# Expert attention: V projection moved behind the last weight transposes, and VectorE's copy of V moved last

## What is computed

```
for e in range(4):                      # experts, 12 heads of 16 each, x is 16 samples x 141 tokens x 192
    q, k, v = x @ wq[e].T, x @ wk[e].T, x @ wv[e].T      # split by heads
    scores = q @ k.T / sqrt(16), masked to 0 <= i - j < 64
    o = softmax(scores) @ v
    outs.append(o @ wo[e].T)
fused = concat(outs); result = silu(fused @ w_gate.T) * (fused @ w_up.T)
```

## Time and profile before

| | us |
|---|---|
| median of 3 runs | 1338.97 (1335.55 to 1340.47) |
| profiled execution, its own time | 1340.07 |
| its span, first to last instruction | 1338.3 |
| TensorE busy: matmuls, weight loads | 1199.4, 972.4 |
| ScalarE, VectorE, GpSimd busy | 769.5, 711.5, 349.3 |
| expert attention, about | 632 to 1208 of the span |

### The profile page before, as it was taken

One profiled execution on the slowest core, in us unless ns is written; L12 is line 12 of the kernel. 1 busy time (PEld: TensorE's weight loads), 2 busy tenths in 40 slices (PEclk: granted clock), 3 DMA queues, 4 the chain that ended last, 5 costly groups with the idle time before them and its releaser, 6 DMA issues. The chain is left out here.

```text
span 1338.3 us, 34162 instructions
## 1 busy us (share of the span) xinstructions
PE 1199.4 (90%) x13220; PEld 972.4 (73%) x13220; DVE 711.5 (53%) x2290; ACT 769.5 (57%) x3346; POOL 349.3 (26%) x477
## 2 busy tenths in 40 slices
PE   6789976999997789996899999999999999995898
PEld 5479944777774456653788888988888888983465
DVE  7344465666666110023666667666666667666100
ACT  2155525677773533302877777777777777773432
POOL 2100023333332000002334433444334433441000
PEclk9789966999996799976999999999999999996799
DMA  7000000000006200001000000000000000000000
GB/s 234 20 1 1 2 1 1 1 2 2 2 2 140 44 1 1 0 1 41 2 2 2 3 2 2 2 3 2 2 2 2 2 2 3 2 2 1 9 19 27
DMA packets 34734, 19.85 MB, mean 15 GB/s; under 512 B 24592, under 2 KB 32016, under 8 KB 34576
## 3 DMA queue, kind: packets, MB, share of 16 engines
q1 hardware_dynamic: 34432, 17.20, 4.8%
q10 hardware_dynamic: 144, 0.49, 0.1%
HBM read 15.12 MB, written 1.77 MB: 13 GB/s over the span
## 5 line engine op out<-in xcount | busy, mean ns | idle before, releaser
L1692 POOL TENSOR_TENSOR e_W<-e_W,e_RS 128x384 f32<-128x384 f32 x256 | 203.8, 827 | 349.6 <-DVE e_RS L1620 349.6
L1563 ACT ACTIVATE e_W<-banks,e_MX 128x128 f32<-128x128 f32 x768 | 268.9, 389 | 18.3 <-DVE e_MX L1608 18.2
L1563 ACT ACTIVATION_READ_ACCUMULATOR e_W<-banks,e_MX 128x1 f32 x768 | 176.1, 229 | 0.0
L1557 ACT COPY e_PT<-banks 128x512 f32<-128x512 f32 x128 | 69.0, 588 | 105.0 <-PE banks L1468 105.0
L1420 PE MATMUL banks<-XT,e_wqk 128*128 128x141 f32 x768 | 112.2, 297 | 11.9 <-DVE e_GU L1662 8.4
L469 POOL TENSOR_TENSOR rstd<-veps,nhalf 128x6 f32<-128x6 f32 x15 | 20.6, 1373 | 365.8 <-DVE veps L435 365.8
L1420 PEld LDWEIGHTS banks<-XT,e_wqk 128*128 128x128 f32 x768 | 98.5, 194 | 14.3 <-issue 11.6
L1468 PE MATMUL banks<-ident,e_W 128*128 128x128 f32 x768 | 105.5, 273 | 2.7 <-POOL e_W L1692 1.6
L1432 PE MATMUL banks<-e_wv,XT 128*128 128x192 f32 (+1 forms) x512 | 100.2, 339 | 0.3 <-ACT e_K L1552 0.2
L1468 PEld LDWEIGHTS banks<-ident,e_W 128*128 128x128 f32 x768 | 90.3, 141 | 6.2 <-POOL e_W L1692 1.9
L1608 DVE TENSOR_REDUCE e_MX<-banks 128x3 f32<-128x384 f32 x128 | 65.4, 553 | 42.8 <-PE banks L1456 42.8
(11 more groups left out here) (245 smaller groups left out, 2743.2 us busy)
## 6 DMA issues: line engine op xcount, KB each, us to landing
xp<-in_patches_dram SPq DMA_DIRECT2D x4, 768.0 KB, 8.2
H<-in_h_dram SPq DMA_DIRECT2D x1, 1728.0 KB, 10.3
out_dram<-H SPq DMA_DIRECT2D x6, 288.0 KB, 2.3
e_g<-in_e_gu_dram SPq DMA_DIRECT2D x1, 1536.0 KB, 8.3
e_o<-in_e_o_dram SPq DMA_DIRECT2D x4, 192.0 KB, 5.9
e_wqk<-in_e_qk_dram SPq DMA_DIRECT2D x8, 96.0 KB, 2.6
e_wqk<-in_e_qk_dram SPq DMA_DIRECT2D x24, 32.0 KB, 2.3
e_wv<-in_e_v_dram SPq DMA_DIRECT2D x4, 192.0 KB, 2.6
```

Source lines behind the costliest of these rows:

```text
L1557: nc.scalar.copy(PT[:, 4 * u:4 * u + 4, :], bank[4 + u][:, 0:4 * P]).then_inc(s_pa, 1)
L1563: ex = nc.scalar.activation(W[n % 2][:, t, :], bank[i][:, x * P:(x + 1) * P], ACT.Exp, bias=MX[:, t:t + 1], accum_out=SM[n % 2][:, t:t + 1])
L1692: nc.gpsimd.tensor_tensor(x, x, RS[n % 2][:, 3 * i:3 * i + 3].unsqueeze(2).broadcast_to([P, 3, P]), ALU.mult).then_inc(s_nm, 1)
```

## The change

On TensorE, project_v(n) moves from directly behind scores(n) to behind transpose(n-1, 2) and transpose_tail(n-1). On VectorE, evacuate_v(n) moves from directly behind maxima(n) to behind the first reciprocal, and evacuate_tail(n-1) moves ahead of that reciprocal.

```diff
@@ TensorE @@
                         if n < N:
                             scores(n)
-                            project_v(n)
                         if 1 <= n <= N:
                             pe.wait_ge(s_pa, 2 * n - 1)
                             pe.wait_ge(s_nm, 5 * n - 1)
...
                             pe.wait_ge(s_pa, 2 * n)
                             pe.wait_ge(s_nm, 5 * n)
                             transpose_tail(n - 1)
+                        if n < N:
+                            project_v(n)
                         if n >= 2:
                             out_project(n - 2)
@@ VectorE @@
                         if n < N:
                             maxima(n)
-                            evacuate_v(n)
                         if 1 <= n <= N:
                             evacuate_weights(n - 1)
+                            evacuate_tail(n - 1)
                         if n < N:
                             reciprocals(n, 0, 6, 2)
-                        if 1 <= n <= N:
-                            evacuate_tail(n - 1)
+                            evacuate_v(n)
                         if n >= 5 and n % EXPERTS == 1:
                             copy_out((n - 5) // EXPERTS)
```

## The result

The changed kernel takes 1319.93 us (median of 4 runs, 1318.65 to 1320.78) against 1337.26 (4 runs); the ratio is 0.9869 with a 95% interval of 0.9841 to 0.9896. That is 17.5 us less by the ratio. Of these 3 us, 1.7 come from the kernel before, whose median is now 1337.26 and was 1338.97 when the range was counted from it. The profiled execution took 1320.78 us, its span 1319.1 (1338.3 before).

A forecast was written before the change was run, and what follows sets the result against it. TensorE was taken to set the pace, so only its pauses could be won: 30 even iterates by 0.35 (10.5) plus 0.6 at the start, 11.1 us, from median 1338.97 to 1327.9 us; range 1323.3 to 1333.

The forecast's parts named there:

- The wait for e_PTT: Attended products wait for VectorE's tail-weights copy; removing this was to gain 0.35 us per even iterate.
- the 0.14 us gap: Between out projection's last load and attended loads: remains with nothing awaited, cutting the even iterate's gain from 0.50 to 0.35 us.
- the slower rival: V's later copies hold up the q/k projection: 22 us more, time 1361; chance 0.04.
- The bound of 0.4 us: Iterate 0's q/k projection, delayed by V's copies, stays covered by the first transposes' wait: charged 0, at most 0.4.
- priced at 0.6: Iterate 1, without out projection, waits 1.21 us for the tail's copy, which comes 0.62 us sooner: 0.6 us gained.
- Iterate 62's gain: Expected lost, because in the last scored iterate, 63, the second transposes already wait for e_ON.
- the block between 904.04 and 905.98: TensorE's V, third set and tail, permuted: zero net, 0.05 us either way per iterate, 3.1 us over 62.
- e_K no longer releases V: Sign to look for: V's projection, moved back on TensorE, no longer starts on the end of k's copies; no size given.
- The bound of 0.05: Uncertainty for new block neighbours on TensorE: 0.05 us either way per iterate, 3.1 us over 62.
- None shows less than no gap: Reading of the nearest trace rows for the new seams on TensorE, used to take zero net cost.
- The cap: Second transposes wait for VectorE's copy e_ON: at most 0.40 us per even iterate; as rival, 6.6 us gained, 1332.4, chance 0.11.
- the range's best case: Low end of the range: even iterates at 0.40 us (12.6) with 3.1 from the seams, 1323.3 us.

The follow-up runs named there:

- the changed kernel's second profile: The changed kernel itself, unaltered, timed once more beside the kernel with VectorE's copy e_ON moved ahead: 1319.58 us, ratio 0.9868.
- the bank freed: Kernel before, with half of k's last copy taken from SBUF instead of PSUM and V's projection waiting only for the two bank-reading copies: 1335.45 us, ratio 0.9972.
- e_ON first: Changed kernel, with VectorE's copy e_ON of the attended values moved ahead of the reciprocal of the tail's sums: 1315.24 us, ratio 0.9841.
- the bank freed with VectorE's order: Kernel before, with VectorE's new order and V's PSUM bank freed one copy earlier, TensorE's order as before: 1325.01 us, ratio 0.9896.

## Why the prediction was wrong

**Direction, mechanism and most steps held.** The wait for e_PTT went from 32 times to iterate 1 and the 0.14 us gap in its place was measured in the even iterate. The Trainium skill's rule of a drain at a change of tiling mode (TensorEngine Tiling (Array Packing), Key Properties) agrees with that gap: it stands in the odd iterates before (in the even ones the longer wait covered it) and in both kinds after. The trace does not show that the rule is the cause: the change back, from the 32-column tiles to the full-array q/k projection, leaves 0.02 us (881.59 + 0.52 = 882.11, then 882.13), and no run took the 0.14 away. V's copies came 0.8 us ahead of the q/k projection, 0.9 was worked out: the slower rival was far off. Iterate 0 cost 0.01 us, charged 0, and here luck had a part. In the changed kernel's second profile its q/k projection, behind the same pause of 3.00 us, ran at a granted clock of 0.50, the 1.2 GHz level, for 2.85 us instead of 1.50, and the masks of iterate 1 came 10.91 us behind those of iterate 0 instead of 9.40. There the projection before it had run at 1.00 instead of 0.50 and had won as much. The bound of 0.4 us had not thought of the clock. Iterate 1 gained 0.76 (17.59 to 16.83 us from the second q/k projection), priced at 0.6; VectorE's order, which the 0.6 was put down to, gave 0.15 of it alone. Iterate 62's gain was lost, as said.

**The step that failed** is the one on the block between 904.04 and 905.98: "I take zero net and keep 0.05 us either way per iterate". It was 0.17 us less in every iterate, 10.5 us over 62. It came in two parts.

1. A wait that the prediction had in its hands and did not price. It said that V "stood right behind" the end of k's copies, 903.99 to 904.04, and used this only as slack gained. But 0.05 us is the time that it had itself found between a copy's end and the start of the loads that wait for it. V was waiting, 0.12 us in each iterate: 7.4 us. The 0.04 us between the tail scores' recorded end and V, which the prediction took for the cost of a change of shape, was the visible rest of this wait: with the bank freed V starts 0.08 us before that end (869.15, against 868.79 + 0.44). That no idle time was named there is no evidence, because the recorded span of the tail scores' loads (0.44 us) ran to within 0.04 us of V's start; in the changed kernel the next load starts 0.34 us after the same group's start, inside that span. The bank-freed run takes the 0.12 us away without touching the order. The trace did name the wait in iterate 1 (0.26 us), and the prediction listed "e_K no longer releases V" as a sign to look for, with no price.
2. Real differences of neighbours, net 0.05 us per iterate, 3 us. The tail scores are followed 0.34 us later by a transpose and 0.36 by V; the third set takes 0.42 us behind the tail scores and 0.49 behind V; V followed by the out projection costs 0.04 to 0.05 more. These are read from the traces; no run separated their causes, and I leave them open. The bound of 0.05 held for this part alone, and its sign was a gain. "None shows less than no gap" was also misread: in the earlier trace rows the third set's recorded end, 905.81, lies behind the tail's start, 905.78.

**The cap.** The prediction put 0.05 us of room before the second transposes meet e_ON. The even iterate gained 0.52 us, 0.35 from e_PTT and 0.17 from above, so the cap did bind, by 0.09, and the pair kept 0.43 of it, near the 0.40 worked out. The sign named for it, the second transposes naming e_ON, could not show: no idle time is printed for the 0.09 us. What the range's best case lacked lies elsewhere. It held the even iterates to 0.40 and added 0.05 per iterate, 15.7 us in all, while the odd iterates, which no cap holds, gained 0.17 each instead of 0.05: 3.7 us over 31. Less 0.02 in each even one, that is the 18.8 us by which the phase shrank.

**The sum as it should have been:** per pair of iterates 0.35 for e_PTT, 2 x 0.12 for k, 2 x 0.05 for the neighbours, less 0.09 for e_ON, is 0.60; 17.71 us became 17.12. Thirty pairs (iterates 2 to 61) give 18.0 us and iterate 1 another 0.8; the phase became 18.8 shorter, the whole execution 17.5 by the ratio.

## What to carry to other kernels

In these traces loads that wait start 0.05 us after the end of what they wait for. An instruction found at that distance may be waiting, whether or not an idle time is shown; compare its distance to its predecessor with an iterate in which that wait cannot occur. When a block is moved away from a producer that ended just ahead of it, price the distance that goes, not only the slack that comes. And a cap found downstream limits only what lies ahead of it in that iterate.

## What the runs showed that was not expected

Recorded spans of weight loads overlap the next load by about 0.1 us (0.44 us recorded, 0.34 us to the next start), so a short wait of TensorE hides in that overlap: the k wait of 0.12 us left 0.04 us between the recorded spans, the e_ON wait of 0.09 us none, and neither was printed as idle time in the steady iterates while together they were worth some 10 us. The two halves of the change are not additive: TensorE's alone costs 16.5 us, VectorE's alone gives 8.6 (6.3 by its trace), both give 17.5. And one pause of 3 us at the start of the phase was followed by the 2.4 GHz level in three profiles (the changed kernel, VectorE's order alone, e_ON first) and by the 1.2 GHz level in two (the changed kernel again, and the bank freed with VectorE's order, where the pause was 3.33 us).
